# Stationary values, transposed attention, and softmax by halves of the heads in a fused block

## What is computed

```
x = x + matmul(fake_quant(layernorm(x)), fake_quant(ctx))        # ctx: 16 x 1024 x 1024
qkv = layernorm(x) @ Wqkv          # 32 heads of 32; one k and one v for all heads
scores = q k^T * scale + alibi     # causal, 64 x 64 for each head
x = x + (softmax(scores) @ v) @ Wo
l = layernorm(x)
r = softmax(l @ gate_w.T)          # 8 experts
x = x + (l * (r @ in_scale)) @ sign(weight).T * (r @ out_scale) + bias
```

## Time and profile before

| | us |
|---|---|
| three runs, median (lowest to highest) | 440.33 (439.89 to 441.54) |
| the profiled execution, time | 441.02 |
| the profiled execution, span of the instructions | 439.2 |

### The profile page before, as it was taken

One profiled execution on the slowest core, in us unless ns is written; L12 is line 12 of the kernel. 1 busy time (PEld: TensorE's weight loads), 2 busy tenths in 40 slices (PEclk: granted clock), 3 DMA queues, 4 the chain that ended last, 5 costly groups with the idle time before them and its releaser, 6 DMA issues.

```text
span 439.2 us, 9643 instructions
## 1 busy us (share of the span) xinstructions
PE 374.1 (85%) x3968; PEld 258.1 (59%) x3968; DVE 309.7 (71%) x591; ACT 258.8 (59%) x309; POOL 95.6 (22%) x116
## 2 busy tenths in 40 slices
PE   0444966996999989998999999998999899967877
PEld 0114936953736956595659655874578457934354
DVE  7678579989846278786888587849885986285242
ACT  4777898747678655765767575756666631243020
POOL 5210010003403203150414032313122121111031
PEclk9999996899899999999999999999999999999968
DMA  7999998699399854775477646874493000000011
GB/s 314 389 398 409 407 395 325 238 364 352 122 370 295 336 179 163 272 228 191 147 271 256 210 145 207 322 218 143 145 307 104 1 39 12 1 1 2 0 45 52
DMA packets 30386, 91.99 MB, mean 209 GB/s; under 512 B 8256, under 2 KB 8512, under 8 KB 30336
## 3 DMA queue, kind: packets, MB, share of 16 engines
q1 hardware_dynamic: 28464, 84.45, 54.4%
q10 hardware_dynamic: 1872, 6.82, 4.2%
HBM read 85.50 MB, written 4.19 MB: 204 GB/s over the span
## 4 chain that ended last, share of the span: by engine, by line
PE 63%; DVE 18%; DMA 7%; ACT 6%; issue 5%; POOL 0%; SPq 0%; DVEq 0%; ACTq 0%
PE R L1651 8%; PE T L1466 7%; PE R L1417 7%; PE R L1419 6%; PE R L1418 6%; PE R L1505 5%; PE R L1507 5%; PE R L1508 5%; DMA ring<-ctx 5%; PE C L1447 4%; ACT b L565 4%; PE T L1603 3%; DVE Pr L1051 2%; DVE st L947 2%; DVE mx L1056 1%
## 5 line engine op out<-in xcount | busy, mean ns | idle before, releaser
L565 ACT ACTIVATE b<-ring,quant,qpar 128x2048 uint8<-128x2048 f32 x64 | 133.0, 2091 | 10.3 <-DMA ring<-ctx 7.6
L1505 PE MATMUL R<-T_hi,Wqkv_hi 128*128 128x128 f16 x448 | 79.1, 222 | 0.0
L1507 PE MATMUL R<-T_lo,Wqkv_hi 128*128 128x128 f16 x448 | 79.0, 222 | 0.0
L1508 PE MATMUL R<-T_hi,Wqkv_lo 128*128 128x128 f16 x448 | 79.0, 222 | 0.0
L1447 PE MATMUL C<-b,aT 128*64 128x512 f16 x256 | 37.1, 416 | 13.7 <-ACT b L565 10.7
L1505 PEld LDWEIGHTS R<-T_hi,Wqkv_hi 128*128 128x128 f16 x448 | 45.1, 101 | 0.4
L318 POOL TENSOR_TENSOR Pr<-Pr,mx 128x512 f32<-128x512 f32 x16 | 16.7, 1043 | 131.0 <-DVE mx L1056 131.0
L1507 PEld LDWEIGHTS R<-T_lo,Wqkv_hi 128*128 128x128 f16 x448 | 44.6, 100 | 0.1
L1508 PEld LDWEIGHTS R<-T_hi,Wqkv_lo 128*128 128x128 f16 x448 | 44.6, 100 | 0.0
L1417 PE MATMUL R<-Wo,attT_hi 128*128 128x512 f16 x112 | 42.5, 380 | 1.7 <-DVE attT_lo L1082 1.7
L1418 PE MATMUL R<-Wo,attT_hi 128*128 128x512 f16 x112 | 42.4, 379 | 0.0
(11 more groups left out here) (169 smaller groups left out, 917.8 us busy)
## 6 DMA issues: line engine op xcount, KB each, us to landing
ring<-ctx SPq DMA_DIRECT2D x64, 1024.0 KB, 6.5
ring<-L_attn_Wo SPq DMA_DIRECT2D x4, 1024.0 KB, 7.6
ring<-L_ffn_weight SPq DMA_DIRECT2D x4, 1024.0 KB, 4.9
Wo<-L_attn_Wqkv SPq DMA_DIRECT2D x7, 544.0 KB, 15.4
X<-x ACTq DMA_DIRECT2D x7, 512.0 KB, 3.9
out<-X ACTq DMA_DIRECT2D x6, 512.0 KB, 2.6
sgn<-L_attn_Wqkv SPq DMA_DIRECT2D x1, 544.0 KB, 18.3
X<-x SPq DMA_DIRECT2D x1, 512.0 KB, 12.8
```

The lines of the kernel that those rows point to most:

```text
L565: e.activation(b8[:, c % BRING, :], ring[:, slot, :], ACT.Identity, scale=qR2, bias=qZ2).then_inc(s_rf[slot], 1)
L1505: e.matmul(dst, hi, rows[0], start=k == 0 and g == 0, stop=False, skip_group_check=True)
L1507: e.matmul(dst, hi, rows[1], start=False, stop=False, skip_group_check=True)
L1508: last = e.matmul(dst, lo, rows[0], start=False, stop=k == KT - 1, skip_group_check=True)
```

## The change

The attention product is turned round. `vbd` (64 columns now, without the ones) is the stationary operand and PT is streamed, 256 columns at a time, into 64 rows of a bank of T. The result comes out as the transposed attention that the projection needs, so `ta` and `attn_rows` are gone, and `o_hi`, `o_lo` (the old `ta_hi`, `ta_lo`) read it straight from T. Since the rows of the transposed result can't be scaled by row sums, P is normalised ahead of its transposes: VectorE sums the exponentials and takes the reciprocals (`row_sum`), GpSimd multiplies (`normalize`).

`scores(s, h)` now makes half of the heads for both sequences, into banks 0 and 1 of R for both halves in steady tiles, so that half 0 can go through softmax while the queries of half 1 are made. The order of Wo's rows on the host and the alibi table follow the new order of heads. All engines' lists are written anew: `opening` and `burst` take the place of `first_half` and `second_half`. The bias is added one step later on GpSimd, `tok` takes all of the norms' rows but norm2's, and `norm0` is cut into `norm0_rows` and `norm0_quant`.

```diff
@@ GpSimd
+            def normalize(t, h, b):
+                e.wait_ge(s_rcp, piece(t, h, b) + 1)
+                e.tensor_tensor(by_head(h, b), by_head(h, b), to_heads(h, b), ALU.mult).then_inc(s_nrm, 1)
@@ VectorE
+            def row_sum(t, h, b):
+
+                e.wait_ge(s_exp, piece(t, h, b) + 1)
+                link(e.tensor_reduce(of_heads(h, b), by_head(h, b), AX.X, ALU.add))
+                e.reciprocal(of_heads(h, b), of_heads(h, b)).then_inc(s_rcp, 1)
-            def attn_rows(s, h, b):
-
-                n = (s.i - 1) * 4 + 2 * h + b
-                e.wait_ge(s_pv, n + 1)
-                at_least(e, s_an, n)
-                u = R[:, 2 * b + h, 0:4 * UNITS].rearrange("p (u w) -> p u w", w=UNITS)
-                link(e.reciprocal(rcp[:, :, :], u[:, :, 2 * D:UNITS]))
...
@@ TensorE
             def query(s, n, ks=range(KT)):
-                if n == 0 and k_low(ks):
+                if k_low(ks):
                     if s.is_step(1):
                         e.wait_ge(s_k, 2)
                         e.wait_ge(s_v, 2)
-                    else:
-                        at_least(e, s_an, s.i * 4)
...
+            def pt(s, h, b):
+                e.wait_ge(s_nrm, piece(s.i - 1, h, b) + 1)
+                transposes(s, f"PT{h}{b}", [heads(h, b)[:, n * P:(n + 1) * P] for n in range(4)], s_PT)
+
+            def pv(s, h):
+
+                m, bank = s.i - 1, bank_for(s, f"O{h}")
+                e.wait_ge(s_v, m + 1)
+                for b in range(2):
+                    emptied(s, f"PT{h}{b}")
                     for x, y in ((0, 0), (0, 1), (1, 0)):
                         for r in range(2):
+                            last = e.matmul(T[64 * r:64 * r + 64, bank, b * 256:(b + 1) * 256],
+                                            vbd[m % 2][x][:, b, :], PT[y][:, b, r * 256:(r + 1) * 256],
+                                            start=x + y == 0, stop=x == 1)
+                    last.then_inc(s_pv, 1)
```

TensorE's new lists of a steady step, which the steps below follow:

```diff
+            def opening(s):
+                context(s.i, 2)
+                ffn(s, 0, low)
+                pt(s, 0, 0)
+                pt(s, 0, 1)
+                ffn(s, 0, high)
+                outscale(s, 0)
+                outscale(s, 1)
+                pv(s, 0)
+                context(s.i, 3)
+                ffn(s, 1, low)
+                project(s, 0, low)
+                pt(s, 1, 0)
+                pt(s, 1, 1)
+                project(s, 1, low)
+                pv(s, 1)
+                ffn(s, 1, high)
+                t1(s)
+                project(s, 0, high)
+                project(s, 1, high)
+
+            def burst(s):
+                kv(s)
+                query(s, 0, low)
+                tk(s)
+                query(s, 0, high[:1])
+                t2(s)
+                query(s, 0, high[1:])
+                router(s)
+                query(s, 1, low[:1])
+                scores(s, 0)
+                query(s, 1, low[1:])
+                router_t(s)
+                query(s, 1, high[:1])
+                inscale(s, 0)
+                inscale(s, 1)
+                query(s, 1, high[1:])
+                if s.next:
+                    context(s.i + 1, 0)
+                    context(s.i + 1, 1)
+                scores(s, 1)
```

1061 lines of the change are left out of this document (435 added, 626 removed).

## The result

The changed kernel takes 470.0 us (median of four executions, 464.7 to 470.7) where the kernel before, measured beside it, takes 440.7: 6.4% slower, ratio 1.0639 with a 95% interval of 1.0559 to 1.0720. The direction was forecast; the size was not. 450.1 was forecast and 437 to 460 given, so +9.8 us stands against +29.

The account below looks back on a forecast made before the run. It took the steady part as bound by TensorE, the start and end by chains across engines. Terms of +4.9, +2.0, +4.5, -0.4, +5.1, -1.9, -2.0, -4.9 and +2.5 gave +9.8 on 440.3: 450.1 us, range 437 to 460.

Parts of the forecast that it names:

- x1 of tile 1: First attention: ScalarE's order and a late last exp make x1 start at 71.6 instead of 66.7, +4.9 us.
- kv and the first query: Tile 1: later copies put kv at 82.1, +2.0 us; the first query then waits for v_lo, +4.5 us.
- k_sb's lateness in tile 2: Tile 2's burst: three convolutions ahead of k_copy; tk waits 2.5 us, t2's second half 2.8; term +5.1.
- the wait for PT_lo at pv(1): Steady tile: PT_lo is copied behind norm0_rows, so pv(1) ends at 18.2 instead of 16.2, a new 2.0 us wait.
- the one for k_lo: Steady tile's burst: t2's second bank must be emptied by k_lo, a new wait of 0.9 us.
- the tail: Last scores to the last normed rows' transposes: 25.9 us instead of 30.8, -4.9 us.
- TensorE's own work: Steady tile: transposes of tok go, 24 products replace 48; TensorE needs 42.5 us a tile.
- that rival: Attention products' weight loads show, 0.4 to 1.5 us a tile, +3 to +12 in all, 453 to 462 us; chance 0.13.
- +2.5, from 0 to +6: Term for TensorE's low granted clock behind waits of 4 to 5 us near 66, 83 and 137.
- more low clock and a start that slips further: Rival: +6 us for the clock instead of 2.5 and +3 for the start, 457 us; chance 0.10.
- the term of -1.9: Four steady tiles: 45.4 us each with the new waits, 181.6 where the trace has 183.5.
- Query to kv of tile 2: From tile 1's first query to tile 2's kv: 63.0 us where the trace has 63.4, -0.4.

Follow-up runs that it names:

- conv7: Changed kernel with ScalarE converting context piece 7 in tile 1 ahead of the last exp and the two PT copies; 467.9 us.
- vfirst: Changed kernel with tile 1's k_copy, v_copy and v_lo ahead of the attention's hi and lo copies and Wo's second piece; 465.0 us.
- kfirst: Changed kernel with tile 2's k_copy, v_copy and k_hi ahead of ScalarE's later convolutions of context 3; 461.5 us.
- ptlo: Changed kernel with VectorE copying PT_lo of half 1 ahead of the next tile's normalised rows instead of behind them; 455.5 us.
- combo: Changed kernel with ptlo, conv7, vfirst, context 2's convolutions earlier, ScalarE's burst reordered, and q_lo(1) and the last tile's q_hi(1) moved; 439.5 us.
- warm: Changed kernel, order untouched, with TensorE's idle waits in the start, tile 2's burst and ahead of pv(1) filled by extra products; 457.9 us.
- best2: combo with the first attention's queues reordered, TensorE waits filled, and tile 1's q_hi(1), q_lo(1), half 0 softmax and GpSimd's subtraction moved ahead; 434.8 us.
- fill8: Changed kernel with eight extra 512-column products ahead of pv(1) in the openings of tiles 3 to 7; 465.3 us.
- gap2: Kernel before the change, with pv(1) in tiles 3 to 7 made to wait for a 1024-column GpSimd multiplication; 461.7 us.
- nonorm: Changed kernel without P's normalisation (row sums, reciprocals, multiplications), so its output is not the reference's; 464.7 us.
- gap1: Kernel before the change, with pv(1) in tiles 3 to 7 made to wait for a 512-column GpSimd multiplication; 450.3 us.

## Why the prediction was wrong

**The direction and the queues were right.** x1 of tile 1, kv and the first query, k_sb's lateness in tile 2, the wait for PT_lo at pv(1) and the one for k_lo, no more wait ahead of outscale, and the tail are where the text put them, most within 1 us. conv7, vfirst, kfirst and ptlo, each of which undoes one named order, removed the named waits or a part of them.

**TensorE's own work was nearly right.** A steady tile without waits and at full clock was put at 42.5 us; combo's TensorE is busy 43.0, 2 us more in four tiles. The attention's products go in pairs 0.11 apart (250.52, 250.63), and the 24 of a tile take 1.46 us where no copy is late (ptlo: 0.68 and 0.78), 1.64 with the late PT_lo. So the weight loads set no slower pace, and that rival falls. By the Trainium skill (TensorEngine Tiling (Array Packing), Restrictions) column tiling turns off the fast weight load. The loads agree in part, 114 to 118 ns here against 99 for the projection's; the stream hides them.

**The step that failed is the clock's.** "I take +2.5, from 0 to +6", and only for the start; the steady tile was priced "at 1.00" while the same text put a new wait of 2.0 us into it. The runs show 14.5 us given back by fillers alone ahead of tile 7 (warm): 7.1 ahead of kv of tile 2, 2.1 in tile 2's burst, 5.3 in the four steady tiles (1.3 each, the 1.7 of the half clock less what the wait for k_lo grew). The whole kernel gains 12.1, since behind that warm loses 2.7 again: 1.7 for its fillers in tile 7's opening, where no wait was, and 0.8 for low clock ahead of the tail's transposes. The trace before had a hint, the 0.67 behind the waits of the start; the text used it for the start alone. The rival "more low clock and a start that slips further" had the mechanism, but its 457 kept it out of the steady tiles as well, and at 0.10 it was too low.

**The second step that failed is the steady tile's gain, the term of -1.9.** With the clock taken away it is +2.3 (warm: 185.8 against 183.54), so the sign was wrong too. Half of the -1.9 never was a gain: 45.4 against the 45.63 that the text starts from is -0.2 a tile, and the other 1.0 is the one long tile in the 183.5 (the 0.91 us wait above). Beyond that, a tile takes 46.4 us at full clock and not 45.4, for three things that the table did not have. TensorE's own work is 0.5 more. pv(1) takes 0.96 instead of 0.78, since its second PT_lo comes late too. And scores half 1 waits 0.44 for q_lo. VectorE's pair of XS_lo copies ahead of q_lo takes 2.13 us, against 1.36 for the two in combo, and GpSimd's subtraction beside it takes 1.42 instead of 1.04:

```profile
229.71 2.13 DVE L876 TENSOR_TENSOR XS_lo<-ln2T,XS_hi 128x512 f16<-128x512 f32 x2
229.87 1.42 POOL L329 TENSOR_TENSOR Pr<-Pr,mx 128x512 f32<-128x512 f32 x1 [13.67 <-DVE mx L1030]
```

The text weighed the Trainium skill's statement that GpSimd and VectorE share an SBUF port and block each other (Advanced Engine Details and Errata, VectorE Performance Modes) for the new multiplications and took nothing; those ran in 1.04 each, and it was the old subtraction, moved, that met VectorE. The rows agree in that both instructions are longer where they overlap; that the port is the cause was not tested apart.

**What the misses add up to.** The sum was +9.8 and the profiled executions differ by 28.9. Of the 19.1 between, the clock is 12.0 (14.5 less the 2.5 taken), the steady tiles at full clock 4.2, the start's and tile 2's queues 1.8, and tile 7 and the end 1.1.

**The rest is small.** Query to kv of tile 2 was put at 63.0 and measures 70.06: the half clock in four pieces (the query's first half 5.07 instead of 2.7, tile 2's first context and projection 1.6 more, FFN 3.41 instead of 1.74) is 5.6 of the 7, so this is the clock once more. The last 22 us, forecast unchanged, are 0.7 longer; behind the 3.06 us wait the router runs at 0.50.

Not settled: what decides whether the clock falls behind a wait of 1.7 to 2.9 us. Equal waits in equal surroundings went both ways, so how much of the clock's share an execution pays is partly luck. And best2's next step, less work on VectorE in the first two tiles, was not tried.

## What to carry to other kernels

A wait put on TensorE's path is to be priced twice, as itself and as the low clock that may follow: in these steady tiles 1.7 us more behind 18 of 29 waits of 1.7 us and up, and nothing behind waits up to 1.65. When an order of queues is planned by hand, the wait that is removed often only uncovers the next one in the same queue, so look for an engine that is busy throughout a stretch (VectorE, 96%, at 105 to 114 in best2) before moving copies. Two kernels that differ in one edit differ by luck of the clock too, so compare the marks ahead of the edit before the whole difference is credited to it. And a good idea in a bad table looks like a bad idea: with its queues in order this change saves 2.4 to 2.6 us a steady tile, where the first order lost 1.9.

## What the runs showed of the hardware

- TensorE's granted clock fell to 0.50 behind 10 of 19 waits of 1.71 us, 5 of 5 of 2.08, 3 of 5 of 2.92, and 0 of 5 of 1.64, in the steady part of these kernels; idle products put into the wait kept it at 1.00 all ten times there (fill8, warm).
- The low clock behind such a wait cost 1.7 us at the spot in the changed kernel (tile 4) and 1.6 a tile in gap2 (4.4 against 2.8 of growth). In nonorm and kfirst steady tiles with the same wait of 1.71 us took 47.7 us with low clock and 46.4 without.
- A VectorE subtraction of two 128x512 parts and a GpSimd one of the same size, overlapping in the changed kernel, were both longer than alone: a pair 2.13 instead of 1.36 us, and 1.42 instead of 1.04.
- GpSimd's in-place multiplication by 1.0 took 2.78 us over 1024 columns (gap2) and 1.50 over 512 (gap1), where an addition of 1024 columns with a broadcast operand took 1.89 (kernel before).
